# The rows of a finished head pair: from the maxima's banks and VectorE to the ring of the scores' banks, ScalarE and GpSimd

## The reference

```python
Q = (x @ Wq.T).reshape(H, b, s, dkh)
K = (x @ Wk.T).reshape(H, b, s, dkh)
V = (x @ Wv.T).reshape(H, b, s, dvh)
scores = jnp.einsum('hbqd,hbkd->hbqk', Q, K)
atten = jax.nn.softmax(scores, axis=-1)
out = jnp.einsum('hbqk,hbkd->hbqd', atten, V).reshape(b, s, -1)
y = out + x
mu = jnp.mean(y, axis=(1, 2), keepdims=True)
var = jnp.var(y, axis=(1, 2), keepdims=True)
return (y - mu) / jnp.sqrt(var + EPS)
```

## Time and profile before

| what | value |
|---|---|
| median of 3 runs | 1012.63 us (1012.16 to 1015.68) |
| the profiled execution's own time | 1011.26 us |
| its span in the profile | 1009.1 us |
| PE busy | 98% |
| DVE busy | 79% of the span |
| ACT busy | 68% |
| POOL busy | 17% |
| chain that ended last | PE 95%, DVE 2% |

### The profile page before, as it was taken

One profiled execution on the slowest core, in us unless ns is written; L12 is line 12 of the kernel. 1 busy time (PEld: TensorE's weight loads), 2 busy tenths in 40 slices (PEclk: granted clock), 3 DMA queues, 4 the chain that ended last, 5 costly groups with the idle time before them and its releaser, 6 DMA issues.

```text
span 1009.1 us, 20754 instructions
## 1 busy us (share of the span) xinstructions
PE 984.5 (98%) x7816; PEld 515.8 (51%) x7816; DVE 800.7 (79%) x1023; ACT 682.0 (68%) x1355; POOL 175.7 (17%) x325
## 2 busy tenths in 40 slices
PE   7999999999998999999999999999999999999995
PEld 6888888888876333333333333333333333333332
DVE  4343455543466899999999999999999999999967
ACT  2212333333322788888888888888888888888884
POOL 2001445444455100000000000000000000000000
PEclk9999999999999999999999999999999999999997
DMA  9967442223300233333333333333334333332204
GB/s 354 369 238 219 138 146 69 74 70 106 101 9 1 59 91 92 94 85 96 89 96 91 91 94 86 100 87 96 89 92 94 86 96 89 97 90 70 73 18 167
DMA packets 127043, 108.59 MB, mean 108 GB/s; under 512 B 81120, under 2 KB 102368, under 8 KB 126944
## 3 DMA queue, kind: packets, MB, share of 16 engines
q1 hardware_dynamic: 122720, 102.81, 35.3%
q10 hardware_dynamic: 4224, 4.46, 1.3%
HBM read 80.75 MB, written 42.21 MB: 122 GB/s over the span
## 4 chain that ended last, share of the span: by engine, by line
PE 95%; DVE 2%; issue 1%; DMA 1%; POOL 1%; SPq 0%; ACT 0%; POOLq 0%; DVEq 0%; ACTq 0%
PE ps L1034 28%; PE ps L1014 23%; PE ps L967 18%; PE ps L999 12%; PE ps L920 5%; PE ps L892 4%; PE ps L908 2%; PE ps L1045 1%; PE ps L1057 1%; DMA wp<-w_out_t 1%; PE ps L881 1%; DVE xn L851 0%; DVE stage L856 0%; DVE stage L870 0%; SPq L292 0%
## 5 line engine op out<-in xcount | busy, mean ns | idle before, releaser
L710 DVE TENSOR_REDUCE negm<-ps 128x1 f32<-128x1024 f32 x512 | 615.1, 1222 | 22.0 <-PE ps L999 14.7
L551 ACT ACTIVATE wp<-ps 128x512 f32<-128x512 f32 x680 | 369.6, 600 | 40.9 <-PE ps L1014 8.1
L1014 PE MATMUL ps<-qf,kf 50*128 50x512 f32 x1024 | 382.7, 449 | 0.0
L999 PE MATMUL ps<-kf,qf 48*128 48x512 f32 x1024 | 360.9, 445 | 0.9 <-DVE negm L710 0.9
L1014 PEld LDWEIGHTS ps<-qf,kf 50*128 50x128 f32 x1024 | 156.8, 185 | 201.9 <-ACT wp L551 107.0
L1034 PE MATMUL ps<-wp,vb 128*17 128x256 f32 x2720 | 212.6, 385 | 0.3 <-issue 0.2
L999 PEld LDWEIGHTS ps<-kf,qf 48*128 48x128 f32 x1024 | 144.1, 185 | 4.3 <-issue 3.9
L551 ACT ACTIVATE picks<-ps 128x512 f32<-128x512 f32 x172 | 103.3, 600 | 21.0 <-PE ps L1014 4.7
L701 DVE SCALAR_TENSOR_TENSOR acc<-ps,gates,acc 128x256 f32<-128x256 f32 x64 | 30.8, 482 | 99.1 <-PE ps L967 95.1
L1034 PEld LDWEIGHTS ps<-wp,vb 128*17 128x17 f32 x2720 | 46.0, 95 | 120.7 <-ACT vstage L551 49.6
L551 ACT ACTIVATE vstage<-ps 128x512 f32<-128x512 f32 x172 | 103.2, 600 | 1.1 <-PE ps L1014 1.1
(11 more groups left out here) (117 smaller groups left out, 821.1 us busy)
## 6 DMA issues: line engine op xcount, KB each, us to landing
qk_d<-stage SPq DMA_DIRECT2D x64, 256.0 KB
feat_d<-qk_d SPq DMA_DIRECT2D x64, 256.0 KB, 3.3
qf<-feat_d SPq DMA_DIRECT2D x128, 128.0 KB
qf<-feat_d SPq DMA_DIRECT2D x128, 64.0 KB
kf<-feat_d SPq DMA_DIRECT2D x128, 64.0 KB
v_d<-vstage ACTq DMA_DIRECT2D x8, 544.0 KB, 5.1
vb<-v_d SPq DMA_DIRECT2D x128, 34.0 KB, 2.4
acc<-x SPq DMA_DIRECT2D x8, 512.0 KB, 7.2
```

Source lines behind the costliest of these rows:

```text
L551: nc.scalar.activation(weight_tile(n, j, b)[:, h * HALF:(h + 1) * HALF], ps[:, ST_BANK[(2 * unit + b) % 3], :], ACT.Exp).then_inc(exp_done, 1)
L710: nc.vector.tensor_reduce(negm[:, n % 2, qt:qt + 1], ps[:, b:b + 2, :].rearrange("p b c -> p (b c)"), AX.X, ALU.max, negate=True).then_inc ...
L999: last = nc.tensor.matmul(ps[:, MAX_BANK[turn % 2] + half, :], qf[rows, u, qt * P:(qt + 1) * P], kf[rows, u, :], start=True, stop=True)
L1014: nc.tensor.matmul(ps[:, ST_BANK[(2 * unit + half) % 3], :], kf[rows, u, j * P:(j + 1) * P], qf[rows, u, h * HALF:(h + 1) * HALF], start=T ...
```

## The change

1. The token rows of a finished pair no longer take a turn of the maxima's banks. They take one turn in the ring of the scores' three banks (`turn_user`, `score_turn`, `row_turn`). Pair 31 alone still uses a bank of the maxima.
2. ScalarE copies the rows to SBUF (`copy_rows`, 128x272, into `rows`, a part of `choice`). GpSimd raises the denominators to the power -1 (128x16), multiplies (128x256) and adds the residual (128x256). VectorE's reciprocal and product remain for pair 31 alone.
3. A unit's order on TensorE becomes scores half 0, scores half 1, maxima half 0, maxima half 1.
4. `pv_out` comes after the exp of half 1 of the fourth unit and not before it; `copy_rows` follows it in odd blocks.
5. One more constant, `minus`, is set at the start.

```diff
@@ -121,6 +121,8 @@
+        rows = choice[:, 0:16 * VW].rearrange("p (g c v) -> p g c v", g=4, c=4)
+        minus = sb("minus", [P, 4, 4])
@@ -201,25 +206,35 @@
+        score_turn, row_turn, turn_user = {}, {}, []
+        for n in range(NB):
+            for unit in range(NKT * n, NKT * (n + 1)):
+                for half in range(2):
+                    score_turn[unit, half] = len(turn_user)
+                    turn_user.append(("exp", 2 * unit + half))
+                if unit == NKT * n + 2 * LAG - 1 and n % 2 == 1 and n > 1:
+                    row_turn[(n - 3) // 2] = len(turn_user)
+                    turn_user.append(("rows", (n - 3) // 2))
+
+        def score_bank(turn):
+            return ST_BANK[turn % len(ST_BANK)]
@@ -396,10 +411,19 @@
             def residual(pair):
-                pool.wait_ge(turn_done, row_turn[pair] + 1)
-                nc.gpsimd.tensor_tensor(xn[:, bass.ds(pair, 1), :].rearrange("p o d -> p (o d)"),
-                                        xn[:, bass.ds(pair, 1), :].rearrange("p o d -> p (o d)"),
-                                        att, ALU.add).then_inc(y_done, 1)
+                tile = xn[:, bass.ds(pair, 1), :].rearrange("p o d -> p (o d)")
+                if pair == NB // 2 - 1:
+                    pool.wait_ge(turn_done, last_turn + 1)
+                    nc.gpsimd.tensor_tensor(tile, tile, att, ALU.add).then_inc(y_done, 1)
+                    return
+                pool.wait_ge(rows_copied, pair + 1)
+                nc.gpsimd.tensor_tensor(rden[:], rows[:, :, :, DH], minus[:], ALU.pow).then_inc(rows_step, 1)
+                pool.wait_ge(rows_step, 2 * pair + 1)
+                nc.gpsimd.tensor_tensor(rows[:, :, :, 0:DH], rows[:, :, :, 0:DH],
+                                        rden[:].unsqueeze(3).to_broadcast([P, 4, 4, DH]), ALU.mult).then_inc(rows_step, 1)
+                pool.wait_ge(rows_step, 2 * pair + 2)
+                tile = xn[:, bass.ds(pair, 1), :].rearrange("p o (c g d) -> p (o g) c d", c=4, g=4)
+                nc.gpsimd.tensor_tensor(tile, tile, rows[:, :, :, 0:DH], ALU.add).then_inc(y_done, 1)
@@ -559,9 +583,16 @@
+            def copy_rows(pair):
+                act.wait_ge(rows_ready, pair + 1)
+                if pair:
+                    act.wait_ge(y_done, pair)
+                nc.scalar.copy(rows, ps[:, score_bank(row_turn[pair]), :].rearrange("p (g c v) -> p g c v", g=4, c=4)[:, :, :, 0:VW]
+                               ).then_inc(rows_copied, 1)
@@ -569,8 +600,10 @@
-                        if (j, h, b) == (LAG - 1, 1, 0) and n:
+                        if (j, h, b) == (LAG - 1, 1, 1) and n:
                             pv_out(n - 1)
+                    if j == LAG - 1 and n % 2 == 1 and n > 1:
+                        copy_rows((n - 3) // 2)
@@ -803,9 +834,7 @@
                     if n % 2 == 1 and n > 1:
-                        if qt == 2 * LAG - 1:
-                            normalise((n - 3) // 2)
-                        elif qt == NKT - 1:
+                        if qt == NKT - 1:
                             statistics((n - 3) // 2)
@@ -843,9 +872,7 @@
-                if c == BATCH - 1:
-                    normalise(NB // 2 - 2)
-                elif c == BATCH:
+                if c == BATCH:
                     statistics(NB // 2 - 2)
@@ -1001,26 +1028,32 @@
+            def free_score_bank(turn):
+                if turn >= len(ST_BANK):
+                    user, count = turn_user[turn - len(ST_BANK)]
+                    if user == "exp":
+                        pe.wait_ge(exp_done, count + 1)
+                    else:
+                        pe.wait_ge(rows_copied, count + 1)
...
-            def crossed_scores(n, j, h):
+            def unit_scores(n, j, h):
                 scores(n, j, h, 0)
+                scores(n, j, h, 1)
                 if n + 2 < NB:
-                    max_scores(n + 2, 2 * j + h, (1,))
-                    max_scores(n + 2, 2 * j + h, (0,))
-                scores(n, j, h, 1)
+                    max_scores(n + 2, 2 * j + h)
```

More of the change, by code:

```diff
@@ L213, in attention_and_experts @@
                     first_turn[0] = next_turn()
-        for n in range(NB):
+        for n in range(NB - 2):
             for qt in range(NKT):
-                if n + 2 < NB:
-                    max_turn[n + 2, qt] = next_turn()
+                max_turn[n + 2, qt] = next_turn()
                 if n == 0 and qt == 2:
                     first_turn[1] = next_turn()
-                if qt == 2 * LAG - 1 and n % 2 == 1 and n > 1:
-                    row_turn[(n - 3) // 2] = next_turn()
-        row_turn[NB // 2 - 1] = next_turn()
+        last_turn = next_turn()
+        score_turn, row_turn, turn_user = {}, {}, []
[9 more added lines that the diff above has]
+            return ST_BANK[turn % len(ST_BANK)]
         def sums_of(t):
@@ L363, in _ @@
             nc.gpsimd.memset(ident[:], 0.0).then_inc(const_step, 1)
-            for value, tile in ((-0.5, mhalf), (EPS, epst), (0.0, zero)):
+            for value, tile in ((-0.5, mhalf), (EPS, epst), (0.0, zero), (-1.0, minus)):
                 nc.gpsimd.memset(tile[:], value).then_inc(const_step, 1)
@@ L719, in normalise @@
             def normalise(pair):
[L720 to L722 removed]
+                o = ps[:, MAX_BANK[last_turn % 2], :].rearrange("p (g c v) -> p g c v", g=4, c=4)
+                dve.wait_ge(turn_ready, last_turn + 1)
+                dve.wait_ge(y_done, pair)
                 nc.vector.reciprocal(rden[:], o[:, :, :, DH]).then_inc(rden_done, 1)
[L724 to L726 removed]
+                dve.wait_ge(rden_done, 1)
                 nc.vector.tensor_tensor(att.rearrange("p (c g d) -> p g c d", c=4, g=4), o[:, :, :, 0:DH],
@@ L1007, in scores @@
                     pe.wait_ge(mrow_in[u], 32 * (n // SLOTS + 1))
-                if unit:
-                    pe.wait_ge(exp_done, 2 * unit - 2 + half)
+                free_score_bank(score_turn[unit, half])
                 if 2 * unit + half < len(ST_BANK):
@@ L1013, in scores @@
                 rows = half_rows(half, SR)
-                nc.tensor.matmul(ps[:, ST_BANK[(2 * unit + half) % 3], :], kf[rows, u, j * P:(j + 1) * P],
+                nc.tensor.matmul(ps[:, score_bank(score_turn[unit, half]), :], kf[rows, u, j * P:(j + 1) * P],
                                  qf[rows, u, h * HALF:(h + 1) * HALF], start=True, stop=True
                                  ).then_inc(st_ready[half], 1)
-            def crossed_scores(n, j, h):
+            def unit_scores(n, j, h):
                 scores(n, j, h, 0)
+                scores(n, j, h, 1)
                 if n + 2 < NB:
-                    max_scores(n + 2, 2 * j + h, (1,))
-                    max_scores(n + 2, 2 * j + h, (0,))
-                scores(n, j, h, 1)
+                    max_scores(n + 2, 2 * j + h)
             def sum_values(n, j, b):
@@ L1040, in to_token_rows @@
             def to_token_rows(pair):
-                turn = row_turn[pair]
                 pe.wait_ge(pv_evac, 2 * pair + 2)
-                free_turn(turn)
+                last_pair = pair == NB // 2 - 1
+                if last_pair:
+                    bank = MAX_BANK[last_turn % 2]
+                    free_turn(last_turn)
+                else:
+                    bank = score_bank(row_turn[pair])
+                    free_score_bank(row_turn[pair])
                 for g in range(4):
-                    last = nc.tensor.transpose(ps[:, MAX_BANK[turn % 2], g * P:(g + 1) * P],
+                    last = nc.tensor.transpose(ps[:, bank, g * P:(g + 1) * P],
                                                ot[:, g, 2 * pair % HELD:2 * pair % HELD + 2].rearrange("p b t -> p (b t)"), ident[:])
-                last.then_inc(turn_ready, 1)
+                last.then_inc(turn_ready if last_pair else rows_ready, 1)
             def maxima_to_rows(n):
```

20 lines of the change are left out of this document (11 added, 9 removed).

## The result

The changed kernel is faster by 0.8%: 1005.51 us median of 4 runs against 1013.67 us for the kernel before in the same comparison, ratio 0.9918 with a 95% interval of 0.9897 to 0.9939. Its profiled execution took 1004.74 us with a span of 1002.9; before it was 1011.26 and 1009.1. So the profiled pair differs by 6.2 us of span, the medians by 8.2.

What follows compares the result with a forecast made beforehand. PE's own sequence was taken to bound the kernel, with gains only in its longer units. 1011.26 - 5.4 - 4.3 - 0.2 + 1.7 = 1003.1 profiled; with the median 1.4 us above, forecast 1004.4 us, range 1001 to 1010.

Steps and rivals of the forecast that it cites:

- What bounds the kernel: In the attention, PE waits for nobody in usual 1.21 us units; only units longer than 1.22 us can be shortened.
- Place one: Fifth unit of odd blocks, behind token rows: maxima wait 0.18 us for a bank; the ring removes it, 5.4 us gained.
- Place two: Behind the copy to `ot`, 31 blocks: late exps make a unit 1.36 instead of 1.22 us; moving the copy gains 4.3.
- The new order: Within a unit on PE: costs nothing; second scores ask 0.11 us earlier for their exp, covered by 0.03 us.
- The rival of the second scores' wait: In every unit, second scores wait for the exp: 1019 us, chance 0.08; smaller bite of 2 to 6 us, 0.12.
- GpSimd: Division in the attention: power 2.84 us, product and sum 0.75 each, 4.5 with handovers; 0.55 to spare before the statistics.
- further margin of 0.5 us: Behind late statistics, VectorE has 0.5 us before the maxima's banks are missed; rival of too slow GpSimd, chance 0.05.
- The tail: After pair 30's transposes the chain is not hidden: VectorE waits for GpSimd's rows, 0.9 + 0.8 = 1.7 us lost.
- 0.2 us of block 62: Same slip behind the copy to `ot`, where ScalarE is the limit: 0.2 us gained.
- The collision of 0.8 us: In the tail, VectorE's work on SBUF lengthens GpSimd's product and sum by 0.42 us each.
- that rival: In the tail, GpSimd and VectorE run strictly one after the other: 3.3 instead of 1.7 us, 1006.0; chance 0.10.

Runs made afterwards that it cites:

- experiment 1: Kernel before, only the division moved: ScalarE copies rows out of the maxima's bank, GpSimd divides; 1014.17 us, ratio 1.0013.
- 3: Changed kernel, but VectorE divides all pairs out of the ring's bank, without ScalarE's copy or GpSimd's division; 1001.65 us, ratio 0.9887.
- Kernel 4: Changed kernel with the unit's order of before (scores 0, maxima 1, maxima 0, scores 1); 1004.86 us, ratio 0.9925.
- 8: Changed kernel with VectorE dividing all pairs out of the ring's bank and the crossed order of before; 1002.09 us, ratio 0.9896.
- experiment 5: Kernel before with only the new order (scores 0, scores 1, maxima 0, maxima 1); 1015.97 us, ratio 1.0028.
- 6: Kernel before with the copy to `ot` moved behind the exp of half 1 and the new order, nothing else; 1002.57 us, ratio 0.9901.
- 2: Kernel before with only the copy to `ot` moved behind the exp of half 1 of the fourth unit; 1007.55 us, ratio 0.9948.
- Experiment 7: Changed kernel with GpSimd made later by an extra power: on 4 elements 1007.54 us, on 16 elements 1136.62 us, one run each.
- first kernel: Changed kernel with one more GpSimd power on 4 elements, 1.08 us more per pair; 1007.54 us, one run.
- second kernel: Changed kernel with GpSimd's power on 16 elements done twice, 2.98 us more per pair; 1136.62 us, one run.

## Why the prediction was right, and where its steps were not

The terms summed to 1003.1 us for a profiled execution; it took 1004.74. The attention brought 2.5 us less than forecast, the rest about 1 us more. That the medians differ by 8.2 us, just the sum of the terms, is luck: the profiled pair differs by 6.5 us.

**What bounds the kernel** held. PE's own sequence sets the pace and VectorE has room: taking 0.68 us per pair from VectorE gave nothing (experiment 1), giving it back cost nothing in the attention (3).

**Place one** had the right size: 1.40 became 1.23 in 30 blocks, 5.1 us for 5.4 forecast. Its cause was told too narrowly. I wrote that the wait goes "with the rows in the scores' ring". It goes so in kernels 4 and 8, but the new order hides it as well, with the turns as they were (5 and 6): the maxima now start 0.34 us into the unit, and the bank is free at 0.18. I had the number for this, and counted only that the maxima's load is asked for 0.11 us later. The change has two remedies for one wait.

**Place two** had the right size as well, 1.36 became 1.23 in 31 blocks. The copy moved alone gave 5.1 us where the step says 4.3: 4.55 in the sixth units of even blocks, which fell to 1.21, and the rest in hundredths over the other units. In the changed kernel the sixth units gave 4.16.

**The new order** was taken to cost nothing, and this term was mis-sized. Even blocks fell from 10.16 to 10.09 us and not to 10.02: their first unit went from 1.21 to 1.25 and others from 1.21 to 1.22 or 1.23. Of the 9.7 us forecast for the attention 7.15 came. Kernel 4 gives back 1.5 us of the rest. Summed unit by unit over blocks 1 to 61, the 2.5 us that are missing lie in two places. The first units of blocks are 1.48 us longer than in the kernel before, and the last units 0.96 us; of these, 0.7 us are two waits for the transfer into `qf`, at the ends of blocks 8 and 32. The first units go with the order: in the kernels with the new one (the change, 3, 5, 6) they are 1.2 to 1.7 us longer than before, in those with the crossed one (1, 2, 4, 8) -0.1 to 0.4 us. Why they are longer stays open. The last units go with neither order (0.2 to 1.0 and 0.0 to 1.5 us). The 0.35 us that came up to block 1 are small against the 3.5 us by which that stretch varies.

**The rival of the second scores' wait** did not come in the changed kernel: in 1.21 us units the load started with the first one's. Its thin cover was real, though. Where the load waits for its exp until 0.38 us into the unit, as in experiment 5, each even block pays the whole of it in the new order (0.39 us) against 0.14 in the crossed one. The new order is safe only because the copy to `ot` was moved with it.

**GpSimd** was priced well by a straight line: the power on 16 elements took 2.93 us on average (2.84), product 0.62 and sum 0.69 (0.75 each). The groups of lines on POOL in the changed kernel (count, busy us, mean ns, idle before), the counterpart of the earlier trace rows:

```profile
L420 POOL TENSOR_TENSOR rden<-choice,minus 128x16 f32<-128x16 f32 x31 | 90.7, 2927 | 149.8 <-ACT choice L594 149.8
...
L426 POOL TENSOR_TENSOR xn<-xn,choice 128x256 f32<-128x256 f32 x31 | 21.2, 685 | 2.4
L422 POOL TENSOR_TENSOR choice<-choice,rden 128x256 f32<-128x256 f32 x31 | 19.3, 623 | 2.4
```

Its timeline at the end of block 25, and VectorE's:

```profile
592.46 2.91 POOL L420 TENSOR_TENSOR rden<-choice,minus 128x16 f32<-128x16 f32 x1 [4.74 <-ACT choice L594]
...
596.15 0.69 POOL L426 TENSOR_TENSOR xn<-xn,choice 128x256 f32<-128x256 f32 x1
```

```profile
597.48 0.42 DVE L764 BATCH_NORM_STATS2 choice<-xn 128x6 f32<-128x256 f32 x1
```

The sum ends at 596.84, 0.64 us before the statistics start (0.55 forecast). The further margin of 0.5 us, until the maxima's banks are missed, was too large: it was taken from a usual unit, and behind the statistics VectorE is later than there. In block 28 the reduction behind the statistics ends at 619.57 and the maxima's load asks at 619.91, 0.34 us later. With the 0.64 us the whole margin is 0.98 us. The forecast's sum of 1.05 is close only because its first part was too small. Experiment 7's expectation counted 1.14, and the 1.08 us of its first kernel already cost PE 0.07 us per pair. The price beyond it, 3 us per 0.1, fits the stalls of the second kernel (2.1 us each for 1.8 expected), but left out the clock.

**The tail** together with blocks 62 and 63 cost 1.3 us; the forecast was 1.7 less 0.2. Right in sum, not in its parts. The 0.2 us of block 62 did not come (0.06 us lost instead). The collision of 0.8 us, 0.42 on each of GpSimd's product and sum, did not come either: they took 0.62 and 0.69 us, their usual lengths, because VectorE stood idle while they ran. The step overlooked that the wait itself takes VectorE out of their way. It was the power that got longer, 3.31 us instead of 2.91. The Trainium skill's rule (SBUF — State Buffer, "Who interferes with whom") is that a VectorE instruction with two inputs in SBUF, or in a two-port mode, and a GpSimd instruction that reads SBUF exclude each other for the whole instruction. The trace does not agree for a power: two instructions of VectorE, of 0.81 and 1.23 us, ran from 982.35 to 984.42, wholly within its 3.31 us and at their usual length, and the second has both inputs in SBUF (`xn` and `acc`). The 1.6 us of that rival did not come.

## What to carry to other kernels

An engine at 96% beside one at 100% need not be its limit: read the starts of the units, look for the ones that are longer than the usual, and price those. A margin is read where the delay arrives, not in a usual unit. When an instruction waits in a fixed order, what counts is what stands behind it: the same late exp cost 0.14 us with the maxima ahead of the waiting scores and 0.39 with them behind. And take a bundle apart before keeping it. Here a moved copy and a swapped order do in two edits what a ring, a copy and a division on a third engine do.

## What was not expected of the hardware

In the kernel with the power twice, PE stalled for about 1.7 us once in two blocks. Behind 17 of 29 such stalls the units ran slowly; behind the stall at 604.85 the granted clock was 0.53 over the next 7 us. Behind the other 12 the units took their usual time, and behind the one at 630.21, of 1.71 us, the clock was 1.00. In those 17 the three units behind cost 2.7 us, more than the 2.2 us of the unit with the stall. Over the whole stretch the slow units and the stalls cost about the same, 58 and 61 us. The 0.18 us waits of the kernel before left the clock at 1.00. A wait that is made longer can so change its price per microsecond. Why one stall is followed by the lower clock and an equal one is not stays open, and all this is from one run.
